# Identity matmuls in TensorE's queue during the first turns of a software pipeline, and a new order of the turn

## The reference, cut to what matters

```
x = x + delta_rule_mixer(layernorm(x))       # 4 heads, recurrence over the tokens, gates from statistics
x = x + cross_attention(layernorm(x), ctx)   # 16 heads of 16 channels, masked softmax over 256 keys
x = x + quantised_ffn(layernorm(x))          # 704 inner channels
```

## Time and profile before

| | |
|---|---|
| median of 3 runs | 1278.31 us (1277.05 to 1282.93) |
| the profiled execution | 1273.96 us |
| its span, first to last instruction | 1272.2 us |
| mean granted TensorE clock over the span | 0.910 |
| PE busy | 1071.3 us (84%) |
| DVE busy | 986.7 us (78%) |
| ACT busy | 749.2 us (59%) |
| POOL busy | 641.7 us (50%) |

### The profile page before, as it was taken

The page is one execution under the profiler, slowest core; times in us unless marked ns, Lnnn a source line. Parts: engine busy times, 40 slices in busy tenths (PEclk is TensorE's granted clock), DMA queues, the critical chain, the costliest instruction groups (busy, mean ns, idle before and its releaser), DMA issues. The chain is left out here.

```text
span 1272.2 us, 27987 instructions
## 1 busy us (share of the span) xinstructions
PE 1071.3 (84%) x8552; PEld 806.0 (63%) x8626; DVE 986.7 (78%) x2955; ACT 749.2 (59%) x1456; POOL 641.7 (50%) x2360
## 2 busy tenths in 40 slices
PE   5888988684677789999999999999999987875755
PEld 4767766683556567777777777777777645443224
DVE  4989988685766869788888888888888776834985
ACT  5877877432343435675666567566656544444766
POOL 4777775405334744565566556556655654101007
PEclk9988889895557869999999999999999998997989
DMA  6667666546021434353353445335343442205007
GB/s 183 214 199 231 197 208 204 180 90 173 34 84 50 121 88 127 105 150 114 93 151 110 132 123 157 115 94 150 109 138 85 145 103 59 76 26 190 1 1 232
DMA packets 159829, 160.31 MB, mean 126 GB/s; under 512 B 65320, under 2 KB 126656, under 8 KB 159680
## 3 DMA queue, kind: packets, MB, share of 16 engines
q1 hardware_dynamic: 155552, 157.47, 41.7%
q10 hardware_dynamic: 4128, 1.05, 0.4%
HBM read 96.34 MB, written 61.87 MB: 124 GB/s over the span
## 5 line engine op out<-in xcount | busy, mean ns | idle before, releaser
L2142 DVE CUSTOM_DVE_ANT_0 x_psA<-x_psA,x_mask_q 128x256 f32<-128x256 f32 x496 | 201.1, 447 | 82.5 <-PE x_psA L1431 59.2
L1694 ACT ACTIVATE x_PT<-x_psB 128x512 f32<-128x512 f32 x240 | 143.2, 596 | 140.8 <-PE x_psB L1458 133.8
L314 DVE SCALAR_TENSOR_TENSOR a_conv<-a_ps_proj,taps,a_conv 128x253 f32<-128x253 f32 (+2 forms) x288 | 114.9, 470 | 12.5 <-ACT a_conv L381 12.5
L537 PE MATMUL a_ps_proj<-a_hT,wqkv 128*128 128x256 f32 x384 | 104.8, 421 | 11.0 <-DVE a_conv L314 7.8
L1431 PE MATMUL x_psA<-x_Ks,x_Qs 96*128 96x256 bf16 x496 | 97.8, 279 | 13.0 <-DVE x_maxima L2142 12.8
L1458 PE MATMUL x_psB<-x_Qs,x_Ks 98*128 98x256 bf16 x480 | 92.7, 274 | 7.3 <-ACT x_PT L1694 2.5
L537 PEld LDWEIGHTS a_ps_proj<-a_hT,wqkv 128*128 128x128 f32 x384 | 77.1, 212 | 30.2 <-issue 15.9
L2142 DVE DVE_READ_ACCUMULATOR2_ANT x_maxima<- 128x1 f32 x512 | 72.2, 141 | 0.0
L1455 PE MATMUL x_psB<-x_mask_k,x_ident_bf 128*128 128x512 bf16 x167 | 64.8, 388 | 8.5 <-ACT x_PT L1694 7.5
L1472 PE MATMUL x_psO<-x_PT,x_V 128*32 128x256 f32 x1024 | 70.3, 393 | 1.6 <-ACT x_PT L1694 1.6
L1431 PEld LDWEIGHTS x_psA<-x_Ks,x_Qs 96*128 96x128 bf16 x496 | 41.4, 101 | 47.0 <-DVE x_maxima L2142 26.8
(11 more groups left out here) (383 smaller groups left out, 3262.5 us busy)
## 6 DMA issues: line engine op xcount, KB each, us to landing
scratch_keypack<-a_keypack SPq DMA_DIRECT2D x16, 768.0 KB, 4.2
c_keypack<-scratch_keypack SPq DMA_DIRECT2D x16, 768.0 KB, 4.9
x_Ks<-scratch_k_parts SPq DMA_DIRECT2D x192, 64.0 KB, 2.7
matrix<-scratch_taps_copies SPq DMA_DIRECT2D x32, 256.0 KB, 4.0
scratch_k_parts<-x_parts_k SPq DMA_DIRECT2D x32, 192.0 KB, 2.3
scratch_q_parts<-x_parts_q SPq DMA_DIRECT2D x32, 192.0 KB, 2.3
x_Qs<-scratch_q_parts SPq DMA_DIRECT2D x32, 192.0 KB, 3.0
a_x_in<-in_x SPq DMA_DIRECT2D x16, 256.0 KB, 3.9
```

The lines of the kernel that those rows point to most:

```text
L314: nc.vector.scalar_tensor_tensor(acc, ps_proj[PROJ_BANK[p]][:, c, 0:L - j], taps[:, p, c, TAPS - 1 - j:TAPS - j], acc, ALU.mult, ALU.add). ...
L537: last = nc.tensor.matmul(ps_proj[PROJ_BANK[p]][:, o], wqkv[:, p, c, o * P:(o + 1) * P], hT[par][:, c], start=c == 0, stop=c == FC - 1)
L1694: nc.scalar.activation(PT[:, k % (2 * GROUP)], bank_B(b, k)[0], ACT.Exp, scale=XD ** -0.5).then_inc(pexp_ready, 1)
L2142: last = nc.vector.tensor_tensor_reduce(bank_A(b, k)[0][:, s], bank_A(b, k)[0][:, s], mask_q[:, t], 1.0, LOWEST, ALU.add, ALU.max, maxima[ ...
```

## The change

At fourteen new steps, `hot0` to `hot13`, PE multiplies an identity by an identity into the bank `psO`, with no semaphore. `HOT` says how many times for each of batches 0 to 4, 173 in all. One such matmul has bf16 operands (the fp32 identity read as bf16 pairs) and 512 columns. `hot0` to `hot9` have stage 0, `hot10` to `hot13` stage 1, so that they run in turns 0 to 5: 12, 41, 40, 42, 34 and 4 of them.

The order of the list is new as well. It begins at another place of the cycle, so many stages are changed by one only because a step now lies on the other side of the turn's start. What changes in the queues:

- PE: `gram0` comes before `out` rather than after it; `a0` comes behind `to`, `wop` and `proj` rather than ahead of them; `qproj` ahead of `b1`; `p1` and `pv2` come between `sA13` and `sA14`, so that between `sA14` and `sA15` only `sB14` and `oT8` are left; `maxT` ahead of `sA0`; `sB0` ahead of `gate1`; `tuh` earlier.
- DVE: `sums3`, `tt` and `att0` come between `mA10` and `delta`, `att1` between `sums2` and `mA13`; `invr` is between `osum` and `osum3`; in turn 0 the transpose of `invb` comes ahead of `tt` and `att0`; `pr3` ahead of `mA6`.
- ACT: `w5` comes ahead of `sq1`, `xd` between `nat0` and `nat1`; `exp` between `w0` and `uc0`.
- POOL: `scale` and `oF` come right behind `stats` and ahead of `rv`; `invb` is first in turn 0.
- SP: `ld_K0`, `ld_Q0` and `ld_Q1` together, `ld_S` behind them, `st_x2` behind `ld_S`.

```diff
--- before.py
+++ after.py
@@ -786,30 +786,37 @@
 
 
 
-C_ORDER = [(2, "rv"), (3, "osum3"), (4, "scale"), (5, "mA10"), (2, "delta"), (1, "invx"), (5, "mA11"), (1, "invq"),
-           (1, "att0"), (4, "oF"), (4, "klow"), (4, "rstdx"), (7, "rstdb"), (4, "qlow"), (3, "ostat"), (5, "mA12"),
-           (2, "sums2a"), (2, "sums2"), (5, "mA13"), (2, "stats"), (3, "st8"), (1, "invb"), (4, "Q1st"), (1, "att1"),
-           (5, "mA14"), (1, "invp"), (1, "invd"), (1, "inva"), (5, "mA15"), (7, "h3"), (4, "mA0"), (5, "sh2"), (4, "mA1"),
-           (2, "st16"), (3, "ogs"), (1, "invs"), (1, "sums0a"), (1, "sums1"), (6, "ot0"), (0, "invk"), (4, "mA2"), (2, "inve"),
-           (1, "sums3a"), (6, "ot1"), (1, "sums1a"), (4, "mA3"), (1, "sums3"), (0, "tt"), (7, "h3m"), (3, "krest"), (4, "mA4"),
-           (1, "sums0"), (6, "x2"), (6, "statb"), (3, "x1"), (3, "ctxT"), (2, "tT"), (4, "sA2"), (6, "tu0"), (2, "gate1"),
-           (6, "tu1"), (5, "sB0"), (3, "kproj"), (4, "sA3"), (1, "a0"), (5, "sB1"), (2, "tTc"), (3, "cTc"), (1, "sqv"),
-           (2, "gelu1"), (5, "eB0"), (3, "khigh"), (5, "eB1"), (6, "ofc"), (3, "oTc"), (1, "sq0"), (1, "ua0"), (5, "eB2"),
-           (5, "eB3"), (1, "w0"), (5, "eB4"), (1, "uc0"), (2, "exp"), (5, "eB5"), (1, "S"), (5, "eB6"), (6, "tuo"), (3, "to"),
-           (4, "sA4"), (5, "sB2"), (6, "wop"), (3, "proj"), (2, "logits"), (5, "sB3"), (1, "b0"), (4, "sA5"), (7, "st_x2"),
-           (5, "ld_S"), (8, "st_h3"), (4, "ld_Q1"), (0, "ld_pack"), (4, "ld_K1"), (3, "st_kp"), (3, "ld_K0"), (0, "ld_vs"),
-           (3, "st_qp"), (2, "ld_x"), (3, "ld_Q0"), (2, "ld_c"), (1, "ld_hT"), (3, "statx"), (4, "mA5"), (2, "pr1"),
-           (2, "pr2"), (4, "mA6"), (2, "pr3"), (1, "r1"), (0, "invr"), (4, "mA7"), (3, "xnx"), (2, "mixa"), (4, "mA8"),
-           (2, "mixb"), (2, "mixc"), (2, "mix"), (3, "qrest"), (4, "mA9"), (2, "osum"), (5, "sB4"), (1, "c0"), (4, "sA6"),
-           (5, "sB5"), (1, "state"), (5, "pv0"), (1, "rhs1"), (4, "sA7"), (5, "sB6"), (1, "a1"), (5, "sB7"), (4, "sA8"),
-           (3, "xT"), (1, "b1"), (5, "sB8"), (3, "qproj"), (4, "K1st"), (4, "sA9"), (5, "sB9"), (1, "c1"), (7, "tuh"),
-           (3, "K0st"), (5, "sB10"), (1, "out"), (4, "sA10"), (0, "gram0"), (4, "sA11"), (5, "sB11"), (5, "pv1"), (4, "sA12"),
-           (5, "sB12"), (0, "gram1"), (5, "sB13"), (4, "sA13"), (5, "pv2"), (5, "sB14"), (4, "sA14"), (2, "oT8"), (5, "sB15"),
-           (0, "p1"), (4, "sA15"), (2, "og1"), (5, "pv3"), (3, "sA0"), (4, "maxT"), (3, "vproj"), (3, "sA1"), (2, "og2"),
-           (0, "p2"), (1, "ua1"), (5, "eB7"), (3, "xTc"), (1, "w1"), (5, "eB8"), (3, "qhigh"), (5, "eB9"), (1, "uc1"),
-           (7, "h3c"), (5, "eB10"), (2, "osq"), (0, "nat0"), (5, "eB11"), (5, "OT0"), (5, "eB12"), (1, "sqd"), (0, "nat1"),
-           (5, "eB13"), (5, "eB14"), (0, "sq1"), (2, "oT8c"), (5, "eB15"), (0, "xd"), (0, "w5"), (2, "gelu2"), (4, "sh1"),
-           (5, "OT1"), (3, "vc"), (2, "oge"), (0, "xur"), (3, "Q0st")]
+C_ORDER = [(2, "r1"), (1, "invk"), (5, "mA7"), (3, "mixb"), (2, "rv"), (4, "klow"), (4, "rstdx"), (7, "rstdb"), (5, "mA8"),
+           (3, "mixc"), (3, "mix"), (4, "qrest"), (5, "mA9"), (3, "osum"), (1, "invr"), (3, "osum3"), (5, "mA10"),
+           (2, "sums3"), (0, "invb"), (1, "tt"), (1, "att0"), (2, "delta"), (5, "mA11"), (2, "sums2a"), (5, "mA12"),
+           (2, "sums2"), (4, "qlow"), (1, "att1"), (1, "invx"), (5, "mA13"), (3, "st8"), (5, "mA14"), (5, "mA15"), (7, "h3"),
+           (1, "invp"), (5, "sh2"), (1, "invq"), (1, "invd"), (4, "mA0"), (1, "inva"), (7, "h3m"), (5, "sA13"), (1, "hot10"),
+           (6, "pv2"), (1, "p1"), (5, "sA14"), (6, "sB14"), (3, "oT8"), (5, "sA15"), (1, "hot11"), (6, "sB15"), (3, "og1"),
+           (5, "maxT"), (4, "sA0"), (1, "hot12"), (6, "pv3"), (4, "Q1st"), (4, "mA1"), (2, "st16"), (3, "ogs"), (2, "inve"),
+           (6, "ot0"), (4, "mA2"), (1, "invs"), (1, "sums1"), (1, "sums3a"), (4, "mA3"), (6, "ot1"), (1, "sums1a"),
+           (1, "sums0a"), (3, "krest"), (4, "mA4"), (6, "x2"), (6, "statb"), (3, "x1"), (4, "vc"), (1, "xur"), (3, "oge"),
+           (3, "cTc"), (2, "tTc"), (2, "gelu1"), (5, "eB0"), (1, "sq0"), (6, "ofc"), (3, "khigh"), (3, "oTc"), (5, "eB1"),
+           (5, "eB2"), (1, "ua0"), (5, "eB3"), (1, "w0"), (2, "exp"), (5, "eB4"), (1, "uc0"), (5, "eB5"), (7, "h3c"), (1, "S"),
+           (5, "eB6"), (1, "sqv"), (5, "eB7"), (4, "vproj"), (1, "p2"), (4, "sA1"), (3, "og2"), (1, "hot13"), (3, "ctxT"),
+           (4, "sA2"), (2, "tT"), (6, "tu0"), (5, "sB0"), (0, "hot0"), (2, "gate1"), (4, "sA3"), (6, "tu1"), (0, "hot1"),
+           (3, "kproj"), (4, "sA4"), (6, "tuo"), (5, "sB1"), (3, "to"), (6, "wop"), (0, "hot2"), (0, "hot3"), (3, "proj"),
+           (5, "sB2"), (1, "a0"), (2, "logits"), (5, "sB3"), (4, "st_kp"), (3, "ld_c"), (2, "ld_hT"), (1, "ld_vs"),
+           (4, "st_qp"), (4, "ld_K0"), (4, "ld_Q0"), (4, "ld_Q1"), (3, "ld_x"), (5, "ld_S"), (7, "st_x2"), (0, "ld_pack"),
+           (4, "ld_K1"), (8, "st_h3"), (3, "statx"), (2, "pr1"), (2, "pr2"), (3, "ostat"), (1, "sums0"), (4, "mA5"),
+           (2, "stats"), (3, "scale"), (3, "oF"), (2, "pr3"), (4, "mA6"), (3, "xnx"), (2, "mixa"), (1, "b0"), (4, "sA5"),
+           (0, "hot4"), (7, "tuh"), (5, "sB4"), (1, "c0"), (4, "sA6"), (5, "sB5"), (1, "state"), (0, "hot5"), (5, "pv0"),
+           (5, "sB6"), (1, "rhs1"), (4, "sA7"), (5, "sB7"), (3, "xT"), (1, "a1"), (5, "sB8"), (4, "sA8"), (4, "K1st"),
+           (3, "K0st"), (3, "qproj"), (1, "b1"), (5, "sB9"), (4, "sA9"), (0, "hot6"), (1, "c1"), (0, "gram0"), (5, "sB10"),
+           (4, "sA10"), (1, "out"), (5, "sB11"), (4, "sA11"), (5, "pv1"), (0, "hot7"), (5, "sB12"), (4, "sA12"), (0, "gram1"),
+           (5, "sB13"), (0, "hot8"), (0, "hot9"), (3, "xTc"), (5, "eB8"), (1, "ua1"), (3, "qhigh"), (1, "w1"), (2, "osq"),
+           (5, "eB9"), (1, "uc1"), (0, "nat0"), (5, "eB10"), (0, "xd"), (5, "eB11"), (5, "OT0"), (5, "eB12"), (1, "sqd"),
+           (0, "nat1"), (5, "eB13"), (5, "eB14"), (2, "oT8c"), (0, "w5"), (0, "sq1"), (5, "eB15"), (4, "sh1"), (2, "gelu2"),
+           (5, "OT1"), (3, "Q0st")]
+HOT = ((0, 0, 2, 0, 0, 0, 0, 4, 0, 6, 0, 8, 3, 6),
+       (0, 2, 0, 0, 3, 4, 4, 0, 5, 6, 1, 0, 8, 7),
+       (1, 1, 0, 0, 7, 5, 5, 4, 1, 0, 8, 2, 7, 7),
+       (2, 0, 0, 4, 4, 8, 0, 0, 0, 0, 7, 0, 0, 0),
+       (2, 5, 0, 0, 5, 4, 0, 6, 0, 5, 1, 0, 0, 3))
 
 LOWEST = -3.0e38
 MASKED_BY_ACT = ()
@@ -1505,6 +1512,11 @@
                         for t in range(TT):
                             last = nc.tensor.transpose(ps_join[:, c * L + t * P:c * L + (t + 1) * P], h3[:, t, c * P:(c + 1) * P], ident[:])
                     last.then_inc(h3_turned, 1)
+                elif op[:3] == "hot" and b < len(HOT):
+                    pair = ident[:].bitcast(BF16)
+                    for _ in range(HOT[b][int(op[3:])]):
+                        nc.tensor.matmul(psO[:], pair[:, 0:P], pair.unsqueeze(1).broadcast_to([P, 2, L]),
+                                         start=True, stop=True, skip_group_check=True)
                 if op == "wop" and b == B - 1:
 
                     pe.wait_ge(fw_step, FW_STEPS)
```

## The result

The changed kernel takes 1261.79 us (median of 4 runs, 1260.29 to 1268.41), the kernel before 1277.68 (4 runs, 1273.14 to 1282.93). The ratio is 0.9884, 95% interval 0.9851 to 0.9917: 15 us less, between 11 and 19. The prediction said 1270 with a range of 1254 to 1287, which holds the result; the narrower range of its own forecast, 1263 to 1277, just misses it.

The account below looks back on a forecast made before the run. PE bounds full turns (43.96 of 44.5 us busy); early turns are a chain between engines at a low clock. Early -16 plus full +8 gives -8 from 1273.96, so 1266, or 1270 for the median; range 1254 to 1287.

Parts of the forecast that it names:

- The early turns, -16: Turns before the full ones: a higher clock and the new order together save 16 us.
- the clock's -13: Turns 1 to 4: added matmuls raise PE's clock, 15 us saved less 2 to 3 us of cost.
- half of the freed time: Turns 2 to 4: half of the PE time freed by a full clock counts as on the path.
- 3 us for `invr`: Turn 1, DVE: `invr` now ahead of `att0` and `delta` gives back some 3 us of 9.
- The factor 0.8: Turns 1 to 4: slow clock rise and the longer `stats` wait leave 0.8 of 19 us, 15.
- 2 to 3 us for the matmuls between the solves: `hot4` to `hot6`: 49 matmuls, 10.8 us, over some 8 us of gaps put 2 to 3 us on the path.
- the clock does not hold: Rival, early turns: matmuls run at the low clock, 21 us land on the path, total 1299; chance 0.07.
- `w5` ahead of `sq1`, -3: Early turns, ACT: `xur` no longer late, `a0` of batch 0 at 301.8 instead of 305.37; taken as -3 us.
- The full turns, +0.7 each: End of the attention scores, `sA12` to `sA15`: PE waits for DVE, +0.7 us in each of eleven turns, +8.
- DVE holds PE up: Rival, `sA12` to `sA15` in every full turn: up to 1.65 us a turn, 18 us, total 1286; chance 0.20.
- The early turns gain and the full turns stay: Rival: early turns save 16 to 21 us, full turns stay at 44.5, total 1260; chance 0.20.
- Nothing measurable: Rival: freed time is lost in waits for `stats` and DVE, gain and loss near 5 us, total 1278; chance 0.10.

Follow-up runs that it names:

- e1: The changed kernel's new order with none of the added matmuls; ratio 1.0017 to the kernel before, median 1276.42 us.
- e2: The kernel before, in its old order, with the same 173 matmuls added behind the same PE steps; 1263.66 us, ratio 0.9911.
- e4: The changed kernel with each added matmul 4 columns wide instead of 512; 1275.40 us in one run.
- e6: The changed kernel up to the end of turn 5, then the remaining steps in the order of before; 1257.09 us, ratio 0.9824.
- e3: The changed kernel with `p1` and `sB15` put back just ahead of `sA15`, and `sB14` ahead of `sA14`; 1266.96 us, ratio 0.9930.
- e8: The changed kernel with `sums3` and `tt` moved earlier on DVE, ahead of `mA8` and behind `mA3`; 1268.29 us, full turns 45.18 us.
- e10: The changed kernel with `p1` alone moved behind `sA14`; 1269.84 us, ratio 0.9967 to the kernel before.
- e11: The changed kernel with only the 49 matmuls of `hot4` to `hot6`, between the solves; 1269.18 us, ratio 0.9967 to the kernel before.
- e5: The kernel before with the 173 matmuls in the old order, plus `w5` ahead of `sq1` on ACT; 1307.30 us, ratio 1.0232.

## Why the prediction was right in its direction and too small

**The mechanism** was as described: the matmuls hold the clock (e1, e2, e4), and the order loses in the full turns more than it gives in the early ones.

**The early turns, -16, were mis-sized.** Measured -29.3, of which 27.2 in turns 1 to 4; with the same queues in e6's execution 25.4 there. Of the two terms in the -16, the order's -3 was -3.7 alone; the clock's -13 was too small: -18.5 for the matmuls alone, -25.6 on top of the new order. The prediction's parts by turn, ahead of its deductions, were at most 6 us in turn 1 (9 less 3 for `invr`) and 5.0, 5.3 and 4.0 in turns 2 to 4, half of the freed time (20.3 in sum, where it writes 19). The changed kernel is 11.0, 4.5, 7.8 and 3.9 us shorter than the one before; set against the order alone, 6.9, 4.9, 7.5 and 3.4. Of the three deductions one was not found and two were:

- *3 us for `invr`*: not found. In turn 1 DVE is through with it, and with `sums3` and `tt`, before `att0` may start: `att0` is released by the end of `out`, after 0.45 us of idle time.
- *The factor 0.8*: about right. The clocks of 1.00, 0.86, 0.96 and 0.96 in place of 0.50, 0.58, 0.67 and 0.78 take away 0.84 of the low-level time, by the prediction's own weights.
- *2 to 3 us for the matmuls between the solves*: right in kind and size, even at the full clock. With the order alone `c0` starts 0.14 us behind the end of `w0` on ACT. In turn 2 `w0` ends at 346.26 and `c0` starts at 347.39, behind seven matmuls. Reckoned so, they cost 0.6 us in turn 1 and 1.9 in turn 2 (an estimate from the starts and ends in the traces).

`att0` of batch 1, then `w0`, the seven matmuls and `c0` of turn 2, in the kernel after:

```profile
320.38 0.69 DVE L1944 TENSOR_TENSOR c_solve<-c_ps_gram,c_causal 128x512 f32<-128x512 f32 x1 [0.45 <-PE c_ps_u L1307]
...
345.88 0.38 ACT L1589 ACTIVATE c_W<-c_ps_w 64x256 f32<-64x256 f32 x1 [1.03 <-PE c_ps_w L1273]
...
345.77 1.68 PE L1518 MATMUL x_psO<-ident 128*128 128x512 bf16 x7
347.39 0.68 PE L1281 MATMUL c_ps_u<-c_W,c_solve 64*64 64x64 f32 x8
```

So what failed is "half of the freed time on the path". By its own reckoning 0.84 of 38 us, 32, were freed, and against the order alone turns 1 to 4 gave 22.7 of them, over two thirds, even with the cost between the solves in it. The bound for a clock held everywhere, -22, is passed too. Another 2.8 us came where the prediction had put nothing: 1.9 in turn 5 and 0.9 between the first `gram0` and `p1` of batch 0. And a part is luck: 197.4 us is the shortest early stretch of all kernels here; e3, e6, e8 and e10, whose early queues of PE are the same but for the places moved at the end of turn 5, have 199.5 to 205.6.

**The rival "the clock does not hold"** was there in places: in turn 1 of e11 as a whole, in a part of turn 1 of e6, where turn 1 of the changed kernel held. The deduction of 0.8 stood for it; what it missed is that a part of such a loss comes out of the next turn's wait for `stats`, 2.5 of 5.5 us in e6.

The Trainium skill, "TensorE: Matmul & The Clock Gate", section "A second HAM failure mode: psum-queue depth-cycling", reports of one kernel that frequent short idle times between groups of matmuls were enough to make its clock swing. By that rule 1.0 in turn 1 could not be counted on; the traces agree in part, with 1.00 in the changed kernel and 0.84 and 0.66 in e6 and e10.

**`w5` ahead of `sq1`, -3**: right in kind and size. From the first `gram0` to `a0` it is 18.0 us before, 14.5 with the order alone, which is 3.5 less; the prediction's 301.8 is 14.5 behind `gram0` too. With the matmuls it is 12.6. That the matmuls ahead of it would use up the gain did not happen, since they ran at the full clock (the eleven behind `p1` in 2.55 us).

**The full turns, +0.7 each**: 0.66 measured (0.5 in the first of them), so +6.4 over ten turns where +8 over eleven was forecast (turn 5 belongs to the early ones). The last `sA` waits as said (0.47 against 0.48). The reason was half right: `sA12` waits 0.20 and `sA13` 0.08 beyond their usual step of 0.22, `sA14` none, where 0.36, 0.13 and 0.16 were forecast, and what holds DVE ahead of `mA11` is `out`, not the sum of 6.9 us (e8). The waits that can be read come to 0.75, less 0.41 at `sB15` in the turn before the change, 0.34. The other 0.3 are steps longer by 0.1 where other neighbours follow one another; no run tells them apart, and this stays open.

**DMAs and the drain**: no wait of a full turn was found that ends with `ld_S` or another moved load; the shorter turn 1 meets a load that was hidden before, 0.69 to 2.06 us at `gram0` of batch 1. The drain is +1.3, within the 3 allowed, and about as much without the new order (+1.2 in e2).

**The rivals.** "DVE holds PE up" has the right place and a third of its price. "The early turns gain and the full turns stay" has the time, 1260, by the wrong half: the early gain was that large, and the full turns did not stay. "Nothing measurable" is what the order alone does; it is not what the change does.

**Do order and matmuls add up?** From `gram0` to `p1` they give 3.7 and 18.5 alone and 29.3 together. But kernels with both and nearly the same early queues lie between 147.7 and 156.4 us in turns 1 to 4, and e10_p1_swap, with 205.6 from `gram0` to `p1`, is 21.1 below the kernel before, less than the 22.2 of the two added up. So all 7 us can be the execution. e5 was to settle it and did not. It stays open.

## What to carry to other kernels

In a pipeline's first turns, where chains between engines leave TensorE half idle, look at the granted clock before counting work: wide matmuls into an idle bank, in the gaps, were worth 18 us there in one execution and 11 us of 1275 by the medians; the same number of narrow ones was worth nothing. They cost little while the clock was up, but not nothing: where a group was longer than its gap, the next product came up to 1.0 us late. An order written for all turns should not be taken whole for the sake of the first ones: switching orders once the pipeline is full brought the short full turn back, 5.9 us over nine turns, at the price of 3.7 at the seam. And a step that looks free on one engine is tied to its places on the others: of six attempts to move a few steps, each argued from the timelines of two engines, one changed nothing and five made the full turn 0.2 to 6 us longer, four of them through a queue that had not been looked at, ACT's or POOL's.

## What the hardware showed that was not expected

The same queues had different clocks: in turn 1 the clock stayed at 1.00 in one execution and fell to 0.54 for 8 us in another, 5.5 us of that turn. And a full turn is not safe from the clock: around one wait of 1.68 us in 48, with PE 96% busy over the turn, the granted clock was 0.76 over 6 us, and the four matmuls behind the wait took 1.73 us instead of 1.03; by the estimate above the low clock cost about as much as the wait itself.
